# Causal attention: the maximum fills of the first slot begun right behind the projections, the last twelve value products dealt out between them

## The reference

```python
x = x + 0.5 * _L0_ffn_ref(_layernorm(x, axis=-1), ...)
x = x + _L0_attn_ref(_layernorm(x, axis=-1), ...)      # the block of the change
x = x + 0.5 * _L0_ffn_ref(_layernorm(x, axis=-1), ...)

# inside _L0_attn_ref, B, T, D, H = 4, 1024, 128, 16 and dh = 8
qkv = (x @ qkv_w.T + qkv_b).reshape(B, T, 3, H, dh)
scores = jnp.einsum('bhtd,bhsd->bhts', q, k) * scale
scores = jnp.where(causal, -jnp.inf, scores)
attn = jax.nn.softmax(scores, axis=-1)
seq_out = jnp.einsum('bhts,bhsd->bhtd', attn, v)
# further down: a linear memory of outer products, gated and added, then out_w
```

## Time and profile before

| | us |
|---|---|
| median of 3 runs | 1920.42 |
| lowest and highest | 1919.04, 1920.77 |
| the profiled execution | 1922.61 |
| span of its trace | 1920.7 |
| mean granted TensorE clock, share of full speed | 0.985 |

### The profile page before, as it was taken

How to read it: one execution, slowest core, us unless ns; L and a number is a source line. 1 busy time by engine, 2 the same in 40 slices (tenths; PEclk the granted TensorE clock), 3 DMA queues, 4 the chain that set the end, 5 groups by cost and what they waited for, 6 DMA issues and landing times. The chain is left out here.

```text
span 1920.7 us, 61287 instructions
## 1 busy us (share of the span) xinstructions
PE 1856.6 (97%) x22646; PEld 1108.6 (58%) x22646; DVE 1603.5 (83%) x5443; ACT 1491.9 (78%) x4110; POOL 929.2 (48%) x568
## 2 busy tenths in 40 slices
PE   7999999999999989999999999889999999999999
PEld 3777774577775443344444448637777635777754
DVE  5899974899995668999999949979999658999945
ACT  4999995699998362777777763469999847999973
POOL 2788861488883050000000036648888405888820
PEclk9999999999999995999999999999999999999999
DMA  6212230122221041111111000002121201222211
GB/s 179 50 44 50 45 70 6 29 47 48 47 54 42 1 151 38 42 41 41 42 41 41 26 7 5 2 20 51 44 51 44 62 6 36 45 50 45 67 23 44
DMA packets 76330, 85.33 MB, mean 44 GB/s; under 512 B 17327, under 2 KB 50803, under 8 KB 75907
## 3 DMA queue, kind: packets, MB, share of 16 engines
q1 hardware_dynamic: 75839, 81.40, 17.0%
q10 hardware_dynamic: 196, 0.02, 0.0%
HBM read 20.83 MB, written 8.39 MB: 15 GB/s over the span
## 5 line engine op out<-in xcount | busy, mean ns | idle before, releaser
L336 ACT ACTIVATE probs<-probs,negmax 128x128 f32<-128x128 f32 x1024 | 401.9, 402 | 2.3 <-DVE negmax L411 1.9
L2328 ACT ACTIVATE gprobs<-ps_global 128x1024 f32<-128x1024 f32 (+3 forms) x384 | 291.5, 811 | 126.2 <-PE ps_global L1765 103.5
L291 POOL TENSOR_TENSOR rot<-rot 128x1024 f32<-128x1024 f32 x128 | 302.5, 2363 | 143.9 <-DVE rot L381 143.9
L297 POOL TENSOR_TENSOR qk<-rot,cnorm 128x1024 f32<-128x1024 f32 x128 | 244.0, 1906 | 173.6 <-issue 150.9
L304 POOL TENSOR_TENSOR probs<-probs,iden 128x1024 f32<-128x1024 f32 x128 | 243.0, 1898 | 47.2 <-DVE iden L419 46.5
L2010 DVE TENSOR_REDUCE maxes<-ps_global 128x1 f32<-128x512 f32 (+2 forms) x384 | 222.1, 639 | 11.6 <-PE ps_global L1728 6.5
L411 DVE CUSTOM_DVE_ANT_0 probs<-ps_attn,masks 128x128 f32<-128x128 f32 x1024 | 226.2, 287 | 0.8 <-issue 0.8
L336 ACT ACTIVATION_READ_ACCUMULATOR probs<-probs,negmax 128x1 f32 x1024 | 204.2, 199 | 0.0
L1723 PE MATMUL ps_global<-kq 48*128 48x512 bf16 (+3 forms) x768 | 197.3, 346 | 7.1 <-DVE maxes L2010 1.8
L2240 POOL CAST m_parts<-m_turn 32x128 bf16<-32x128 f32 x16 | 4.5, 282 | 364.7 <-DVE m_turn L2024 364.7
L377 DVE TENSOR_TENSOR rot<-ps_attn,rotary 128x512 f32<-128x512 f32 x256 | 175.1, 684 | 1.8 <-PE ps_attn L202 1.5
(11 more groups left out here) (235 smaller groups left out, 4501.5 us busy)
## 6 DMA issues: line engine op xcount, KB each, us to landing
v_first<-v_second SPq DMA_DIRECT2D x256, 128.0 KB, 2.3
hs<-z_a SPq DMA_DIRECT2D x256, 32.0 KB, 1.9
ln<-z_b SPq DMA_DIRECT2D x56, 128.0 KB, 2.4
kq<-split_scratch SPq DMA_DIRECT2D x64, 96.0 KB
kq<-split_scratch SPq DMA_DIRECT2D x64, 64.0 KB
split_scratch<-parts SPq DMA_DIRECT2D x8, 384.0 KB, 4.3
split_scratch<-gprobs SPq DMA_DIRECT2D x6, 384.0 KB, 4.0
x_tok<-in_x_dram SPq DMA_DIRECT2D x4, 512.0 KB, 5.8
```

What stands on the lines that cost most here:

```text
L291: nc.gpsimd.tensor_tensor(a, a, b, ALU.add).then_inc(C["rot_sum"], 1)
L297: nc.gpsimd.tensor_tensor(qk[:, k % 2, :].rearrange("p (h d) -> p h d", d=DH), rot_a[:, k % 2, :, :], cnorm[:, k % 2, :].unsqueeze(2).to_b ...
L336: last = nc.scalar.activation(probs[:, k % 2, slot, :], probs[:, k % 2, slot, :], ACT.Exp, scale=-1.0, bias=negmax[:, k % 2, slot:slot + 1 ...
L2328: nc.scalar.activation(probs[:, step % RING, 2 * p:2 * p + 2, 0:w], ps[:, S0 + 2 * p:S0 + 2 * p + 2, 0:w], ACT.Exp).then_inc(C["p2_exp"], 1)
```

## The change

Three edits, all in `global_attention_pass`. On PE the value products of chunks 5, 6 and 7 no longer stand ahead of the first fill: after fills 3, 4, 5 and 6 comes one product of chunk 5 each, after fills 9 to 12 one of chunk 6 each, after fills 15 to 18 one of chunk 7 each. PE's wait for the freed value bank stands before the first product of a chunk, the signal `pj_v` to ACT behind the fourth. DVE's wait for all copies of the values is gone; PE takes the same wait ahead of the first `scores`. No product, no transfer and no buffer is added or taken away; the order of DVE, ACT, POOL and SP is otherwise as it was.

```diff
-            def project_values(m):
-                wait(pe, "oo_stage", 2)
-                wait(pe, "pj_v_read", m)
-                for t in range(4):
+            def project_values(m, tiles=range(4)):
+                if tiles[0] == 0:
+                    wait(pe, "oo_stage", 2)
+                    wait(pe, "pj_v_read", m)
+                for t in tiles:
                     c = column(m) + t * TILE
                     last = nc.tensor.matmul(ps[:, VALUES, t * TILE:(t + 1) * TILE], y[:, c:c + TILE], A["wv"][:, :],
                                             start=True, stop=True)
-                last.then_inc(C["pj_v"], 1)
+                if tiles[-1] == 3:
+                    last.then_inc(C["pj_v"], 1)
...
-            for m in range(CHUNKS - BEHIND, CHUNKS):
-                project_values(m)
             wait(pe, "ln_out", CHUNKS)
             for use in range(FILLS + AHEAD):
                 produce(use)
+                late, t = divmod(use - RING, 6)
+                if 0 <= late < BEHIND and t < 4:
+                    project_values(CHUNKS - BEHIND + late, range(t, t + 1))
+            pe.wait_ge(C["pj_v_read"], C.after("pj_v_read", CHUNKS))
             for p in range(2):
                 scores(0, 0, p)
...
-            dve.wait_ge(C["pj_v_read"], C.after("pj_v_read", CHUNKS))
             nc.vector.memset(ps[:, O0, :], 0.0).then_inc(C["bank_set"], 1)
```

## The result

| | before | changed |
|---|---|---|
| median of 13 runs each, us | 1919.89 | 1923.69 |
| lowest and highest, us | 1918.11, 1922.52 | 1921.84, 1927.80 |
| ratio to before | | 1.0024, 95% interval 1.0017 to 1.0031 |
| profiled execution and span, us | 1922.61, 1920.7 | 1924.97, 1923.1 |

The change makes the kernel slower, by 3.8 us in the medians. The forecast was 1.9 us faster. The stage begins some 1 us earlier in this trace, so I measure from the start of the last projection product (708.7 before, 707.7 after): the first scores begin 42.5 us behind it before (751.2) and 46.9 us behind it in the changed kernel (754.6). The loss of 4.4 us lies between these two marks.

The account below looks back on a forecast made before the run. DVE's wait for ACT's value copies, then the takes, were taken as the bound. Wait gone -2.7, fill 0 +0.1, products at half clock +0.7 gave -1.9 us: 1918.5 us, range 1915.9 to 1921.4 for 8 in 10.

Parts of the forecast that it names:

- What bounds the kernel now: First slot's start: DVE idles 2.78 us for ACT's last value copy; then takes are the bound until the first scores.
- Fill 0: First slot's first fill: waits for its load, landing taken as 713.5, done at 714.3; cost 0.1 us.
- A product of two records 0.43: Value product among the fills at half clock: 0.43 us, with a 512-column fill 0.86, above a take's 0.6.
- at full clock the product hides wholly, cost 0: Value products among the fills: fill and product take 0.43 us at full clock, below a take's 0.6.
- low-clock case: Fills 0 to 19 with twelve products all at half clock: 14.3 us of PE work, take 20 0.7 us later.
- The clock comes back because PE works without waiting: Among fills and products: clock returns 3.4 to 6.7 us after 713.5, keeping a lead of 1.85 to 1.2 us.
- The rival that the clock stays low: Half clock through the products among the fills: kernel 0.7 us slower, 1921.1; chance 0.15.
- The load was not late: Rival at the first slot's load: fill 0 at 715.0 leaves some 0.6 us gain, 1919.8; chance 0.10.
- The change did what it says: Rival that something other than the copies held DVE at 716.71, so the change does nothing: 1920.4; chance 0.03.
- More back from the clock: Rival around the first scores: full clock sooner gains 1.7 up to 4.5 us, 1916.8 to 1914; chance 0.10.
- The range: Whole kernel's forecast time, 8 in 10: 1915.9 to 1921.4 us.
- worst case: Clock at half through fill 19, the products priced at 0.43 us each: kernel 0.7 us slower, 1921.1.

Follow-up runs that it names:

- e6: e4 plus twelve unused fp32 products of 128 rows, one at each of the change's places among the fills; ratio 1.0007 to the kernel before.
- e7: e4 plus twelve unused bf16 products of 48 rows and 512 columns at the change's places; ratio 0.9979 to the kernel before.
- e9: e4 plus twelve unused bf16 products of 128 rows and 512 columns at the change's places; ratio 0.9993 to the kernel before.
- e10: e4 plus twelve unused fp32 products of 48 rows and 128 columns at the change's places; ratio 0.9985 to the kernel before.
- e8: e4 plus an unused bf16 product of 48 rows and 512 columns behind each fill from 3 to 58; ratio 0.9992 to the kernel before.
- e1: Kernel before with only DVE's wait moved to PE ahead of the first scores, value products still ahead of the first fill; ratio 0.9997.
- e4: Changed kernel with value products of chunks 5 to 7 back ahead of the fills, into banks 1, 2 and 3; ratio 0.9983 to before.
- e11: e4 plus an unused bf16 product of 128 rows and 512 columns behind each fill from 3 to 58; ratio 1.0006 to the kernel before.

## Why the prediction was wrong

**What bounds the kernel now** was right: DVE was held by ACT's last copy, and with that wait gone take 0 came 2.6 us earlier. The takes were the bound in the kernel before, and what was lost up to the first scores the kernel lost: 4.4 us there, 3.8 us in the medians.

**Fill 0** was right: forecast 4.8 us behind the last projection (713.5), measured 5.0 (712.67). PE idled, and the first fills ran at half clock, as written.

**"A product of two records 0.43"**, and with it "at full clock the product hides wholly, cost 0", is the step that failed first. I took the product's price from rows in which such products follow each other and used it for products that stand alone among bf16 fills. Measured there: 0.83 us at half clock and 0.52 at full (with a fill of 512 columns 0.73, above a take's 0.6), and e6, e7, e9 and e10 show that the extra comes with weights of 128 rows between fills of 48, and not from fp32 alone. Twelve times 0.40 is 4.8 us of PE time in a stretch that PE then bounds. With 0.83 in the same sum the low-clock case would have been 0.7 + 4.8 = 5.5 us slower; it came out 4.4. Most of the rest is that fills of different rows overlap a little where they follow each other: fills 0 to 3 took 2.13 us (712.67 to 714.80) in place of 2.56, fills 13 to 15 0.96 us (724.35 to 725.31) in place of 1.28.

**"The clock comes back because PE works without waiting"** failed too. The clock stayed at half for 51 us, although PE was busy 10.00 of 10.00 us in the middle, and e8 repeats that. The stretches from which I took the step also held products of 128 rows, where the fills have 48; but the changed kernel had such products too, behind four of six fills, and its clock did not come back. What brings it back is open. The rival that the clock stays low was the one that happened, and I had given it 0.15 and priced it at 0.7 us. The rule of the Trainium skill on cycling through PSUM banks ("TensorE: Matmul & The Clock Gate", section "A second HAM failure mode: psum-queue depth-cycling") pointed that way, but no trace here shows the swing that it describes: in the kernel before (719.2 to 760.1), where the prediction said that the trace agrees, and in the changed one it is one unbroken stretch at half clock.

**The other rivals.** The load was not late beyond the forecast. The change did what it says (e1 alone could not be told from before, because the products ahead then hold fill 0). More back from the clock: e4's half clock ended 5.5 us sooner behind the last projection than before's, in the one execution each that was profiled, which is no proof.

**The range** ended at 1921.4, set by the wrongly priced worst case.

## What to carry to other kernels

Price a matmul beside its new neighbours, not in the row where it stands with its own kind: here weights of 128 rows between products of 48 rows were not loaded behind the running product, at 0.11 us for each load of bf16 and 0.40 us in all for a lone fp32 product, so move such products in groups or into a gap. Before interleaving work, look for the gap that the move itself opens: here PE then waited 3.5 us for a load, enough for the 2.8 us of products that had been moved away, and two PSUM banks that are free at that point (e4_banks) gave the whole gain. PE busy all the time is no sign that its clock is full or will come back.

## What the runs showed of the hardware that was not expected

- A lone fp32 128x128 product among bf16 fills of 48 rows costs 0.83 us at half clock and 0.52 at full; four in a row 2.01 us at half clock. With a fill of 512 columns a bf16 product of 128 rows and 512 columns takes 1.08 us at half clock (e9) and 0.64 at full (e11), where the columns alone are 0.86 and 0.43; with 48 rows, bf16 or fp32, the pair stays within the takes' pace of 0.64 to 0.65 us at half clock (e7, e10), less than its columns.
- Weight loads of 128 rows are hidden behind running products of 128 rows (a load of 0.19 us in every 0.43, before), but not where weights of 128 and of 48 rows take turns.
- The granted clock stayed at half for 41 us with PE busy 10.00 of 10.00 us on 48-row products (e8), and at full through the same stretch with every second product on 128 rows (e11), in the executions that were profiled. The latter kernel had two kinds of run, 1913.7 to 1916.8 us at a mean granted clock of 0.996 to 0.997 and 1941.5 to 1947.2 us at 0.977 to 0.979.
